# In-place remainders, a longer ring and fewer unsplit units in the adjacency sweeps of a graph layer

## The reference

```python
h = relu(layernorm(x))
x = x + (adj.T @ h) / adj.sum(axis=0)[:, None]      # sweep 1: message and degrees
h = relu(layernorm(x))
x1 = silu(adj @ h @ W + b)                          # sweep 2
x2 = silu(adj @ x1 @ W + b)                         # sweep 3
return x + x2
```

## Time and profile before

| | |
|---|---|
| median of 3 runs (lowest, highest) | 655.73 us (652.41, 656.75) |
| the profiled execution, its span | 652.93 us, 651.1 us |
| PE busy | 627.9 us, 96% |
| POOL busy | 561.6 us, 86% |
| DVE busy | 504.2 us, 77% |
| ACT busy | 298.8 us, 46% |
| HBM read, mean rate over the span | 197.26 MB, 306 GB/s |
| granted TensorE clock, mean | 0.991 of full speed |

### The profile page before, as it was taken

How to read it: one execution, slowest core, us unless ns; L and a number is a source line. 1 busy time by engine, 2 the same in 40 slices (tenths; PEclk the granted TensorE clock), 3 DMA queues, 4 the chain that set the end, 5 groups by cost and what they waited for, 6 DMA issues and landing times.

```text
span 651.1 us, 6791 instructions
## 1 busy us (share of the span) xinstructions
PE 627.9 (96%) x2232; PEld 403.4 (62%) x2232; DVE 504.2 (77%) x518; ACT 298.8 (46%) x372; POOL 561.6 (86%) x283
## 2 busy tenths in 40 slices
PE   7899999999999989999999999999999999999896
PEld 5355666567565456566667667666666666666563
DVE  3988889878847879687778777777787977976882
ACT  1475433643432164645445445445444445443452
POOL 2399799499796569998999999999999999998794
PEclk9899999999998989999999999999999999999999
DMA  8999999999999999999999999909999999999971
GB/s 272 356 374 332 344 342 365 307 329 366 320 260 328 323 347 336 307 330 284 347 348 310 348 347 322 287 1 211 309 347 335 327 337 323 334 342 304 331 210 33
DMA packets 155827, 199.82 MB, mean 307 GB/s; under 512 B 5520, under 2 KB 138896, under 8 KB 155792
## 3 DMA queue, kind: packets, MB, share of 16 engines
q1 hardware_dynamic: 91568, 136.07, 66.8%
q10 hardware_dynamic: 64224, 63.32, 32.9%
HBM read 197.26 MB, written 2.10 MB: 306 GB/s over the span
## 4 chain that ended last, share of the span: by engine, by line
PE 73%; DMA 16%; POOL 3%; DVE 3%; issue 2%; SPq 2%; ACT 1%; DVEq 0%; POOLq 0%; ACTq 0%
PE dg L393 20%; DMA raw<-in_adj_dram 16%; PE m_ps L316 14%; PE dg L410 9%; PE dg L399 9%; PE dg L400 9%; PE m_ps L336 3%; PE m_ps L321 3%; PE m_ps L322 3%; DVE turned L660 2%; POOL at_lo L778 2%; PE m_ps L419 2%; PE tp L364 1%; POOL a_lo L764 1%; SPq L230 1%
## 5 line engine op out<-in xcount | busy, mean ns | idle before, releaser
L778 POOL TENSOR_TENSOR at_lo<-turned,at_hi 128x1024 fp32r<-128x1024 f32 x160 | 379.5, 2408 | 20.5 <-ACT at_hi L511 11.4
L660 DVE STREAM_TRANSPOSE turned<-raw 128x1024 f32<-128x1024 f32 x256 | 302.3, 1222 | 79.5 <-PE dg L393 46.8
L511 ACT ACTIVATE at_hi<-turned 128x1024 fp32r<-128x1024 f32 x160 | 169.3, 1061 | 201.3 <-DVE turned L660 152.8
L393 PE MATMUL dg<-turned,f_w 128*128 128x512 f32 x384 | 182.1, 597 | 2.2 <-issue 2.2
L764 POOL TENSOR_TENSOR a_lo<-raw,a_hi 128x1024 fp32r<-128x1024 f32 x62 | 145.9, 2388 | 32.3 <-ACT a_hi L480 32.3
L616 DVE TENSOR_TENSOR dg<-raw,dg 128x2048 f32<-128x2048 f32 x60 | 137.6, 2293 | 38.0 <-DMA raw<-in_adj_dram 35.8
L399 PE MATMUL dg<-at_hi,f_hi 128*128 128x512 f32 x320 | 133.9, 418 | 2.0 <-ACT at_hi L511 2.0
L410 PE MATMUL dg<-at_lo,f_hi 128*128 128x512 f32 x320 | 130.2, 488 | 1.0 <-POOL at_lo L778 1.0
L400 PE MATMUL dg<-at_hi,f_lo 128*128 128x512 f32 x320 | 126.4, 395 | 0.0
L316 PE MATMUL m_ps<-raw,h 128*128 128x512 f32 x264 | 120.1, 601 | 6.3 <-DMA raw<-in_adj_dram 6.3
L393 PEld LDWEIGHTS dg<-turned,f_w 128*128 128x128 f32 x384 | 72.7, 190 | 57.7 <-issue 49.5
(11 more groups left out here) (50 smaller groups left out, 251.2 us busy)
## 6 DMA issues: line engine op xcount, KB each, us to landing
raw<-in_adj_dram SPq DMA_DIRECT2D x64, 1024.0 KB, 7.8
raw<-in_adj_dram SPq DMA_DIRECT2D x120, 512.0 KB, 11.4
raw<-in_adj_dram ACTq DMA_DIRECT2D x120, 512.0 KB, 12.4
x<-in_x_dram SPq DMA_DIRECT2D x16, 128.0 KB, 8.1
out_dram<-zs SPq DMA_DIRECT2D x12, 128.0 KB, 14.5
h<-in_x_dram SPq DMA_DIRECT2D x1, 768.0 KB, 9.5
h<-in_x_dram SPq DMA_DIRECT2D x1, 256.0 KB, 3.3
out_dram<-zs SPq DMA_DIRECT2D x4, 64.0 KB, 1.8
```

The costliest lines, as they stand in the source:

```text
L393: mm = pe.matmul(acc, f_w[:, UC * WHOLE3.index(j) + c], turned[:, unit % TURN, c], start=first and c == 0, stop=False)
L511: act.activation(at_hi[:, s % RING3], turned[:, unit % TURN], ACT.Copy).then_inc(hi3_done, 1)
L660: dve.transpose(dst, src).then_inc(t3_done, 1)
L778: pool.tensor_tensor(at_lo[:, s % RING3], turned[:, unit % TURN], at_hi[:, s % RING3].bitcast(f32), ALU.subtract).then_inc(lo3_done, 1)
```

## The change

- The split of the neighbour sweeps: 4 of 16 units are whole instead of 6 (`WHOLE3`). Twelve are split.
- The remainder of a split unit is written over the turned unit itself: `at_lo` and `turned` are the same bytes. The ring has nine places (`TURN = 9`), begins at place 4 (`TURN_OFF`), and a split unit's place is free when PE has multiplied the remainder (`rest3_done`). `at_hi` has 4 places (`RING3`). ACT's rounding still waits for the main product and the remainder of the split unit that had the place. A remainder no longer waits for `rest3`.
- PE multiplies the remainder two units after the unit (`REST_LAG = 2`), not one.
- In even groups 2 and in odd groups 3 of the 12 split units (`DVE_EVEN`, `DVE_ODD`) are turned into PSUM (`dg[:, 1]`, one place for all), and DVE makes their remainder into the ring, three units after turning (`DVE_LAG`), from PSUM and `at_hi`. Two semaphores replace `lo3_done`.
- In sweep 3 SiLU writes to `m_ps` and the residual reads it there; `xw` waits for the residual of the pair before.
- `w` and `bias` move into the overlaid part and are loaded in the loop of the units, at unit 7, on ACT's queue; PE waits for `w` at the first `xw`. `u` has six tiles instead of eight, the tiles lie in another order, and `hi3` waits once more (`deg_added`) at its first use.

The core of the diff:

```diff
-WHOLE3 = (0, 3, 6, 9, 12, 15)
+WHOLE3 = (0, 5, 10, 15)
+DVE_EVEN, DVE_ODD = (3, 13), (3, 8, 13)
+DVE_LAG = 3
-TURN = 5
-RING3 = 3
+TURN = 9
+TURN_OFF = 4
+REST_LAG = 2
+RING3 = 4
...
+        turned = sb("turned", [P, TURN, UC, GROUP], into=whole_tiles)
+        whole_tiles.close()
+        at_lo = sb("at_lo", [P, TURN, UC, GROUP], f32r, into=sweep2)
         raw3[0] = sb("raw3_0", [P, GB, BC], into=sweep2)
...
+        def by_dve(unit):
+            n, q = PIECES[unit // QU]
+            return q * QU + unit % QU in (DVE_ODD if n % 2 else DVE_EVEN)
+
+        def wait_lo3(eng, unit):
+
+            mine = [s for s in splits3 if by_dve(s) == by_dve(unit)]
+            eng.wait_ge(lo3_dve if by_dve(unit) else lo3_pool, mine.index(unit) + 1)
+
+        def lo3(eng, unit):
+            s = split3(unit)
+            eng.wait_ge(hi3_done, s + 1)
+            return eng.tensor_tensor(at_lo[:, place(unit)], turned_tile(unit), at_hi[:, s % RING3].bitcast(f32),
+                                     ALU.subtract)
+
+        def place(unit):
+
+            return (unit + TURN_OFF) % TURN
+
+        def turned_tile(unit):
+
+            if by_dve(unit):
+                return dg[:, 1, :].rearrange("p (m r) -> p m r", m=UC)
+            return turned[:, place(unit)]
...
                 if whole3(back):
                     eng.wait_ge(main3_done, back + 1)
                 else:
-                    eng.wait_ge(lo3_done, split3(back) + 1)
+                    eng.wait_ge(rest3_done, split3(back) + 1)
+            elif place(unit) < TURN_OFF:
+
+                eng.wait_ge(rest1_done, len(splits1))
+            if by_dve(unit):
+                earlier = [s for s in splits3 if by_dve(s) and s < unit]
+                if earlier:
+                    wait_lo3(eng, earlier[-1])
+                else:
+                    eng.wait_ge(degs_ready, QUARTERS)
...
             for unit in range(UNITS3):
                 main3(unit)
-                if unit > 0 and not whole3(unit - 1):
-                    rest3(unit - 1)
+                if unit >= REST_LAG and not whole3(unit - REST_LAG):
+                    rest3(unit - REST_LAG)
...
                 if s >= RING3:
                     act.wait_ge(main3_done, splits3[s - RING3] + 1)
-                    act.wait_ge(lo3_done, s - RING3 + 1)
-                act.activation(at_hi[:, s % RING3], turned[:, unit % TURN], ACT.Copy).then_inc(hi3_done, 1)
+                    wait_lo3(act, splits3[s - RING3])
+                act.activation(at_hi[:, s % RING3], turned_tile(unit), ACT.Copy).then_inc(hi3_done, 1)
...
-                act.activation(z, z, ACT.Silu).then_inc(silu_done, 1)
+
+                dst = z if r < QUARTERS else m_tiles(r, part)
+                act.activation(dst, z, ACT.Silu).then_inc(silu_done, 1)
...
-                dve.tensor_tensor(y, y, x[:, q * QT:(q + 1) * QT][:, m], ALU.add).then_inc(y_ready, 1)
+                dve.tensor_tensor(zs[:, r % 2, m], m_tiles(r, part), x[:, q * QT:(q + 1) * QT][:, m], ALU.add)\
+                   .then_inc(y_ready, 1)
...
+                if by_dve(unit - DVE_LAG):
+                    lo3(dve, unit - DVE_LAG).then_inc(lo3_dve, 1)
...
-                s = split3(unit)
-                pool.wait_ge(hi3_done, s + 1)
-                if s >= RING3:
-                    pool.wait_ge(rest3_done, s - RING3 + 1)
-                pool.tensor_tensor(at_lo[:, s % RING3], turned[:, unit % TURN], at_hi[:, s % RING3].bitcast(f32),
-                                   ALU.subtract).then_inc(lo3_done, 1)
```

More of the change, by code:

```diff
@@ L76, in build @@
         ident = sb("ident", [P, P])
-        w = sb("w", [P, P])
-        bias = sb("bias", [P, P])
         ones = sb("ones", [P, 2])
@@ L392, in main3 @@
                     for c in range(UC):
-                        mm = pe.matmul(acc, f_w[:, UC * WHOLE3.index(j) + c], turned[:, unit % TURN, c],
+                        mm = pe.matmul(acc, f_w[:, UC * WHOLE3.index(j) + c], turned[:, place(unit), c],
                                        start=first and c == 0, stop=False)
@@ L444, in _ @@
                     xw(pair_of(ended))
+            for unit in range(UNITS3 - REST_LAG, UNITS3):
+                if not whole3(unit):
+                    rest3(unit)
             xw(GROUPS - 1)
@@ L721, in _ @@
                     residual(pair_of(ended))
+            for unit in range(UNITS3 - DVE_LAG, UNITS3):
+                if by_dve(unit):
+                    lo3(dve, unit).then_inc(lo3_dve, 1)
             for part in parts(GROUPS - 1):
```

66 lines of the change are left out of this document (37 added, 29 removed).

## The result

| | before | after |
|---|---|---|
| median (lowest, highest), us | 654.38 (652.41, 656.75), 4 runs | 647.96 (645.35, 648.86), 4 runs |
| ratio of the two | | 0.9894 (95%: 0.9845 to 0.9942) |
| the profiled execution, its span, us | 652.93, 651.1 | 648.86, 647.1 |

The change makes the kernel 1.06% faster; 647.0 was forecast. The number came out as predicted, but several of the steps that led to it did not, and the gain comes in part from elsewhere.

The account below looks back on a forecast made before the run. PE was taken to bound nearly everything, DMA the end by a small margin. Earlier restart 6.5, residual 0.7 and fewer whole units at the end 0.6 made 7.8 us: 645.1 or 647.9, named 647, range 643 to 652.

Parts of the forecast that it names:

- Unit prices: Neighbour sweeps: whole unit 1.72 us on PE, split 1.40; DVE's remainder 1.2, residual about 1.2, PSUM transpose unchanged.
- Transfers have no more to give; an earlier issue doesn't move their end: Sweep 2: DMA is full from its start, so transfers still end at about 421.3 us; supply averages 324 to 335 GB/s.
- Rival 1: PE sets the end: DMA delivers more when asked, all of PE's 11.5 us plus 1.7 idle come, 639.7 to 642.5; chance 0.20.
- The restart 6.8 us earlier is worth 6.5 at the end: Pause between sweeps: DVE finishes piece 32 at 431.9 instead of 438.7 us, so transfers restart 6.8 earlier; 6.5 taken.
- DMA is full again and runs as long as before: From the restart to the piece that stopped PE, DMA takes its old time, so the earlier start carries through, 6.5 us.
- PE's start waits gain 1.3 us: Sweep start: PE's small waits for POOL hide in one more unit before the remainder is multiplied, 1.3 us less.
- ACT at nothing: ACT, busy 24 to 25 of 50 us, takes more roundings, moved loads and new waits at no cost.
- met: DVE's wait for ACT's rounding should cost nothing, since it needs PE's main product of a split unit five units away.
- DVE's waits for transfers: Neighbour sweeps: they grow from 17 to 40 us or more and begin in sweep 2.
- PE's waits in the last pair: Sweep 3: PE would stand still for some 5 us where it stood 1.7.
- Rival 2: No gain: a slow DMA stretch of 205 to 230 GB/s grows or recurs, costing the 7.8 us; 652.9 to 655.7; chance 0.23.
- Rival 3: Slower: DVE becomes the bound if its remainder takes 2.7 us, 53.7 us a pair, about 680 us; chance 0.12.

Follow-up runs that it names:

- half the bytes: Transfers of pieces from number 4 on carry half their rows: in the changed kernel 638.53 us, ratio 0.9783; in the kernel before 649.83 us, 0.9949.
- experiment 4: Also "queue order": early norm, plus ACT copying finished groups one unit later and DVE's bias and residual two units later; 643.3 us, ratio 0.9854 to before.
- early norm: Changed kernel with POOL's scale and shift of the last quarter moved from unit 15 to unit 12; 645.95 us, ratio 0.9887 to before.
- ACT's loads earlier, stores shared: Experiment 4 plus ACT's loads one unit earlier and half of sweep 3's eight early-group stores on ACT; 643.77 us, ratio 0.9874 to before.

## Why the prediction was right, and where it was not

- **Unit prices: right.** Whole to split 0.32 us a unit: 8.2 us in six pairs against 7.7 (1.2 a pair in sweep 2, 1.6 in sweep 3). Remainder by DVE 1.19 us against 1.2, transpose into PSUM unchanged, residual from PSUM 1.20 instead of 2.72.
- **"Transfers have no more to give; an earlier issue doesn't move their end": failed.** It was read from a share of 1.10 as "full". DMA gave 336 and 343 GB/s when PE asked for more, and 342 to 346 with the queue order mended. Rival 1 was right up to 590 us: PE took all that it was shortened by. It was wrong about the last pair, where half the bytes still win 5.4 us.
- **"The restart 6.8 us earlier is worth 6.5 at the end": the first half nearly right, the second failed**, and it carried most of the sum. Counted from the beginning of the sweeps DVE was done with piece 32 5.6 us earlier, but ACT's half of the next piece was issued only 1.9 us earlier, since a wait in ACT's queue stood before the issue. The kernel of experiment 4, which restarts where the prediction had it, gains 1.5 us in the table and 2.2 by the ratio over the one it builds on, not 6.5. "DMA is full again and runs as long as before" is the step that doesn't hold. Full at a share of 1.1 is 212 GB/s while one queue moves and 347 while both do. And a buffer comes free at PE's pace: from 430 to 550 us DVE waited 8.9 us for PE and 1.2 us for transfers in experiment 4's kernel. That an early lead of the transfers is lost in this way is argued from these waits, not tested.
- **"PE's start waits gain 1.3 us" and ACT at nothing: failed.** 1.24 us of waits between 260 and 270 us before became 4.5, and about 1.3 of half clock behind them. The rounding that the remainder waits for was "met" by counting PE's distance; it wasn't met because other things stood ahead of it in ACT's queue: the issue of two transfers, the wait for POOL's scale and 5.4 us of ReLUs. The prediction listed what ACT's share was and not what its queue waits for. The ring's own gain there (3.2 us in one execution) is hidden under it.
- **DVE's waits for transfers**: 40 us or more from sweep 2 on were foretold; they are 21.0 us in 24 waits. PE's waits in the last pair: some 5 us forecast, rows of 3.1 us seen, 5.4 by comparison with half the bytes.
- **Rival 2 (slow stretches)** named a true thing without a cause. What is shown is that in the long one behind the pause one queue moves at a time, with transfers issued on the other; why, stays open. The last pair is 2.2 us longer than before, not the 7.8 that would have undone the gain. **Rival 3** didn't come with the PSUM operand, and comes without it (17 us).

So the number was hit by luck: the errors cancelled. PE's gain of 8.2 us in the pairs was real and not in the sum; of the sum's 7.8 us the 6.5 from the restart were mostly not real. Not settled: how much of the medians' 6.4 us is the ring's and how much the split's, with all bytes loaded, and why the end of sweep 1 differs by up to 8.6 us between the executions of the table.

## What to carry to other kernels

Read DMA by queue: where one of two queues moves nothing the other doesn't take up its share (212 GB/s against 347 here), so don't give all small-packet transfers to one queue. Before calling a queue empty, look whether it has transfers issued. Compare times of two profiles from a common event, here the beginning of the sweeps, and not from the beginning of the program. When an instruction is costed as "its input is long there", list what stands before it in its engine's queue and what each of those waits for, at the start of a sweep as in its middle; a share of 50% says nothing about it. Undo one part of a change at a time: here nothing of the gain was left without one line (the lag of two), and the headline part (fewer unsplit units) brought none that could be measured until the transfers were out of the way.

## What of the hardware was not expected

- One hardware queue of 1 KB packets gives 212 GB/s at a share of 1.12, two give 347 at 1.10. The busy share of the DMA engines doesn't show how much they could move.
- With transfers issued on both queues, one queue can move alone: ACT's issue of 440.8 us had no packet under way from 441 to 444, at 214 GB/s.
- The issue of two transfers of the same size took ACT 0.86 us before (at 257.5) and 3.03 after (at 257.3), and what stands behind it in ACT's queue waits: with "early norm" the issue ends at 258.7 and the next instruction starts at 258.8, though its input is there since 255.4.
- A VectorE instruction with two SBUF inputs slows the GpSimd beside it too: 2.40 to 2.61 us on the mean of 152, with 40 such instructions in 430 us.
- PE's granted clock was 0.51 for some 3 us after a stall of 4.2 us, which added 1.3 us to it, and 0.50 for 6 us after one of 2.8 us with `REST_LAG = 1`. The length of a stall didn't decide it: after one of 1.96 us (ACT's loads earlier, stores shared) the clock was 0.57 from 577 to 581 us, after one of 2.12 us (queue order) it stayed at 1.00.
- A 128x1024 fp32 transpose by VectorE into PSUM costs what it costs into SBUF, 1.226 and 1.218 us.
